# One pass for the gate mix, a normalised x kept in place, and the second layer norm on ScalarE from tile 3

## The reference, cut to what matters

```python
# x: (8, 512, 16, 16); tokens: 8 batches of 256, each of 512 channels
v = _ln_c(x)                                   # (x - mean) / sqrt(var + 1e-6), over a token's channels
xf = v.reshape(b, c, h * w)
u = stack([mean(xf), max(xf), std(xf, ddof=1)]) # per batch and channel
med = median(u.reshape(b, -1))                  # per batch
z = einsum('bck,ck->bc', (u - med) ** 3, cfc_w) / sqrt(1 + BN_EPS) * bn_w + bn_b
x = x + v * sigmoid(z)[:, :, None, None]        # the gate mix
t = tokens of x
h = _ln_t(t)                                    # the second layer norm, eps 1e-5
t = t + sum over the one chosen expert of sigmoid(logit) * glu(h, w1, v1, w2) + glu(h, shared weights)
```

## Time and profile before

| | us |
|---|---|
| time, median of 3 runs (414.07 to 414.93) | 414.22 |
| profiled execution, first to last instruction (span) | 411.6 |
| TensorE busy with matmuls in it | 385.1 |
| TensorE busy with weight loads | 303.8 |
| VectorE busy | 258.2 |
| ScalarE busy | 161.2 |
| GpSimd busy | 134.6 |

### The profile page before, as it was taken

The page is one execution under the profiler, slowest core; times in us unless marked ns, Lnnn a source line. Parts: engine busy times, 40 slices in busy tenths (PEclk is TensorE's granted clock), DMA queues, the critical chain, the costliest instruction groups (busy, mean ns, idle before and its releaser), DMA issues.

```text
span 411.6 us, 6789 instructions
## 1 busy us (share of the span) xinstructions
PE 385.1 (94%) x1982; PEld 303.8 (74%) x1986; DVE 258.2 (63%) x475; ACT 161.2 (39%) x274; POOL 134.6 (33%) x186
## 2 busy tenths in 40 slices
PE   5875659999999999999999999999999999999994
PEld 2442238888888788887888888888888888888883
DVE  6997876555857865656875557547375744676322
ACT  3996852223344324211116245153254515354110
POOL 7787811000100100005030245425535442446201
PEclk9998999999999999999999999999999999999999
DMA  8900502011201561140041469726546773752210
GB/s 321 397 2 0 204 1 78 27 51 60 90 30 53 187 247 53 53 153 27 32 133 41 128 217 323 282 98 256 204 134 219 294 258 118 262 182 71 86 37 30
DMA packets 14763, 55.96 MB, mean 136 GB/s; under 512 B 2575, under 2 KB 2575, under 8 KB 11280
## 3 DMA queue, kind: packets, MB, share of 16 engines
q1 hardware_dynamic: 9936, 40.93, 28.0%
q0 software_dynamic: 4800, 14.69, 10.0%
HBM read 43.02 MB, written 13.63 MB: 138 GB/s over the span
## 4 chain that ended last, share of the span: by engine, by line
PE 81%; DVE 7%; ACT 5%; issue 3%; POOL 2%; DMA 1%; DVEq 0%; POOLq 0%; ACTq 0%
PE GU L1255 47%; PE yb L1255 22%; PE th L1247 4%; PE tx L1240 4%; ACT tiles L534 2%; PE th L1284 2%; DVE search_junk L806 1%; ACT scratch L545 1%; ACT scratch L549 1%; DMA x_sb<-x_tok 1%; PE mb L1255 1%; DVE x_sb L864 1%; DVE tiles L862 1%; DVE bn_parts L871 1%; PE mb L1233 0%
## 5 line engine op out<-in xcount | busy, mean ns | idle before, releaser
L1255 PE MATMUL GU<-w_parts,xT 128*128 (+1 forms) x864 | 213.6, 395 | 0.0
L1255 PEld LDWEIGHTS GU<-w_parts,xT 128*128 128x128 f32 x864 | 158.3, 188 | 31.4
L1255 PE MATMUL yb<-w_parts,hT 128*128 (+1 forms) x420 | 102.6, 392 | 0.0
L1255 PEld LDWEIGHTS yb<-w_parts,hT 128*128 128x128 f32 x420 | 77.8, 188 | 15.7
L605 ACT ACTIVATE hT<-th 128x512 fp32r<-128x512 f32 x36 | 21.6, 599 | 170.8 <-PE th L1247 170.8
L472 POOL DMA_INDIRECT out<-x_sb,scatidx x20 | 37.6, 1879 | 92.5 <-DVE x_sb L1098 85.6
L922 DVE TENSOR_TENSOR w_parts<-w_raw,w_parts 128x2048 f32 (+1 forms) x24 | 54.9, 2288 | 7.4 <-issue 7.2
L907 DVE TENSOR_TENSOR hidden<-hidden,GU 128x512 f32<-128x512 f32 x36 | 24.8, 688 | 40.2 <-PE GU L1255 40.1
L522 ACT ACTIVATE w_parts<-w_raw 128x2048 f32 (+1 forms) x24 | 45.2, 1910 | 4.2 <-issue 3.9
L446 POOL TENSOR_TENSOR x_rstd<-x_mv,eps 128x1 f32<-128x1 f32 x16 | 3.0, 190 | 113.4 <-DVE x_mv L874 113.4
L901 DVE TENSOR_TENSOR hT<-th,hT 128x512 fp32r<-128x512 f32 x36 | 24.8, 689 | 23.9 <-ACT hT L605 23.6
(11 more groups left out here) (233 smaller groups left out, 339.8 us busy)
## 6 DMA issues: line engine op xcount, KB each, us to landing
w_raw<-weights SPq DMA_DIRECT2D x27, 1024.0 KB, 5.3
x_sb<-x_tok SPq DMA_DIRECT2D x8, 512.0 KB, 6.5
xn_d<-tiles SPq DMA_DIRECT2D x16, 256.0 KB, 2.0
z_d<-x_sb SPq DMA_DIRECT2D x16, 256.0 KB, 2.0
tiles<-xn_d,tokidx POOLq DMA_INDIRECT x20, 4.7
x_sb<-z_d,tokidx POOLq DMA_INDIRECT x20, 5.5
out<-x_sb,scatidx POOLq DMA_INDIRECT x20, 6.8
conv<-conv_par SPq DMA_DIRECT2D x1, 10.0 KB, 9.0
```

Source lines behind the costliest of these rows:

```text
L1255: last = pe.matmul(dst, left[:, lp, kc, :], wset(q, k, wp, kc), start=(i == 0), stop=(i == 3 * KC - 1))
```

## The change

`tok_std` = (var + eps) * rstd, the token's standard deviation, is a new small tile that GpSimd makes in `token_rstd`, behind `tok_shift`; a new semaphore `std_a` tells of it. `token_norm` writes the normalised tile over x itself instead of into the ring. Since x = v * std + mean, the mixed x less its mean is v * (gate + std): `mix_tile` is now one `scalar_tensor_tensor`, (gate row + std) * v. The mean does not matter to the second layer norm; it is added later, in `add_shared`, which becomes a `scalar_tensor_tensor` (yb + mean + x). The 16 `norm_a` of ScalarE are gone. The second norm of tiles 0 to 2 stays on VectorE; from tile 3 on it is an activation on ScalarE (scale rstd, bias -mean * rstd), for which GpSimd makes the bias (`x1_shift`, two more small instructions in each `rstd_tile`, and a wait on the new semaphore `x1_less`). In ScalarE's order the norm of `first` stands ahead of `h_hi(n)`, and that of the second tile behind `x_hi(first)`.

```diff
             def token_norm(b):
                 act.wait_ge(rstd_a, b + 1)
-                if b >= 2:
-                    act.wait_ge(aT_ready, b - 1)
                 for t in (2 * b, 2 * b + 1):
-                    act.activation(tiles[:, t % RING, :], x_sb[:, t, :], ACT.Identity, bias=tok_shift[:, t:t + 1],
+                    act.activation(x_sb[:, t, :], x_sb[:, t, :], ACT.Identity, bias=tok_shift[:, t:t + 1],
                                    scale=tok_rstd[:, t:t + 1]).then_inc(a_ready, 1)
...
-                own(pool.tensor_scalar(r, tok_mv[:, 2 * b:2 * b + 2, 1], LN_C_EPS, None, ALU.add))
-                own(pool.tensor_tensor(r, r, powers[:, 0, 0:2], ALU.pow))
+                std = tok_std[:, 2 * b:2 * b + 2]
+                own(pool.tensor_scalar(std, tok_mv[:, 2 * b:2 * b + 2, 1], LN_C_EPS, None, ALU.add))
+                own(pool.tensor_tensor(r, std, powers[:, 0, 0:2], ALU.pow))
                 pool.tensor_tensor(m, m, r, ALU.mult).then_inc(rstd_a, 1)
+                pool.tensor_tensor(std, std, r, ALU.mult).then_inc(std_a, 1)
...
             def rstd_tile(t, u):
                 pool.wait_ge(stats_b, t + 1)
-                r = x1_rstd[:, u:u + 1]
+                r, m = x1_rstd[:, u:u + 1], x1_shift[:, u:u + 1]
                 pool.tensor_tensor(r, x1_mv[:, u, 1:2], eps[:, 0:1], ALU.add).then_inc(x1_eps, 1)
+                if t < PREPARED_FIRST:
+                    pool.wait_ge(x1_eps, t + 1)
+                    pool.tensor_tensor(r, r, powers[:, 0, 0:1], ALU.pow).then_inc(rstd_b, 1)
+                    return
+                pool.tensor_scalar(m, x1_mv[:, u, 0:1], -1.0, None, ALU.mult).then_inc(x1_less, 1)
                 pool.wait_ge(x1_eps, t + 1)
-                pool.tensor_tensor(r, r, powers[:, 0, 0:1], ALU.pow).then_inc(rstd_b, 1)
+                pool.tensor_tensor(r, r, powers[:, 0, 0:1], ALU.pow).then_inc(x1_less, 1)
+                pool.wait_ge(x1_less, 2 * (t - PREPARED_FIRST + 1))
+                pool.tensor_tensor(m, m, r, ALU.mult).then_inc(rstd_b, 1)
...
-            def norm_a(t, u):
+            def norm_tile(t, u):
                 if t >= RING:
                     act.wait_ge(xn_out[u], 16 * (t // RING))
                     act.wait_ge(tx_done, t - RING + 1)
-                bias, scale = (v[:, t:t + 1] if isinstance(t, int) else v[:, ds(t, 1)] for v in (tok_shift, tok_rstd))
-                act.activation(tiles[:, u, :], tile_of(x_sb, t), ACT.Identity, bias=bias, scale=scale).then_inc(a_again, 1)
+                act.wait_ge(rstd_b, t + 1)
+                act.activation(tiles[:, u, :], tile_of(x_sb, t), ACT.Identity, bias=x1_shift[:, u:u + 1],
+                               scale=x1_rstd[:, u:u + 1]).then_inc(xn_ready, 1)
...
-            norm_a(0, 0)
-            norm_a(1, 1)
-            norm_a(2, 2)
-            norm_a(3, 3)
...
             for n in range(NT - 1):
                 now = PREPARED[n] if n < len(PREPARED) else ()
-                soon = PREPARED[n + 1] if n + 1 < len(PREPARED) else ()
+                for t in now[:1]:
+                    norm_tile(t, t % RING)
                 h_hi(n, n % 2)
                 silu_gate(n + 1, (n + 1) % 2)
                 for t in now[:1]:
                     x_hi(t, t % RING)
-                for t in soon:
-                    if t >= RING:
-                        norm_a(t, t % RING)
+                for t in now[1:]:
+                    norm_tile(t, t % RING)
...
             def mix_tile(t, u, batch):
-                buf, xt = tiles[:, u, :], tile_of(x_sb, t)
-                dve.wait_ge(a_again, t + 1)
+                xt = tile_of(x_sb, t)
+                dve.wait_ge(std_a, batch + 1)
...
-                dve.tensor_tensor(buf, buf, gate_rows(batch), ALU.mult).then_inc(gate_used, 1)
-                dve.wait_ge(gate_used, t + 1)
-                dve.tensor_tensor(xt, xt, buf, ALU.add).then_inc(x1_ready, 1)
+                dve.scalar_tensor_tensor(out=xt, in0=gate_rows(batch), scalar=tok_std[:, t:t + 1], in1=xt,
+                                         op0=ALU.add, op1=ALU.mult).then_inc(x1_ready, 1)
...
-                dve.tensor_tensor(xt, xt, yb[:, :], ALU.add).then_inc(y_used, 1)
+                dve.scalar_tensor_tensor(out=xt, in0=yb[:, :], scalar=tok_mv[:, t, 0:1], in1=xt,
+                                         op0=ALU.add, op1=ALU.add).then_inc(y_used, 1)
...
                 for t in held if n else ():
                     x_lo(t, t % RING)
-                norm_tile(first, first % RING)
                 take_logits(n, yb)
                 h_lo(n, n % 2)
                 for t in second:
                     gate_tile(t, t % RING, t // 2)
                 gated(n + 1, (n + 1) % 2)
                 x_lo(first, first % RING)
-                for t in second:
-                    norm_tile(t, t % RING)
```

More of the change, by code:

```diff
@@ L109, in program @@
         tok_shift = sb("tok_shift", [P, NT])
+        tok_std = sb("tok_std", [P, NT])
         x1_mv = sb("x1_mv", [P, RING, 2])
         x1_rstd = sb("x1_rstd", [P, RING])
+        x1_shift = sb("x1_shift", [P, RING])
         neg_mean = sb("neg_mean", [P, B, KC // 2])
@@ L155, in program @@
         rstd_a = sem("rstd_a")
+        std_a = sem("std_a")
         a_ready = sem("a_ready")
@@ L183, in program @@
         gates_spread = sem("gates_spread")
-        gate_used = sem("gate_used")
         warmed = sem("warmed")
-        a_again = sem("a_again")
         x1_ready = sem("x1_ready")
@@ L190, in program @@
         x1_eps = sem("x1_eps")
+        x1_less = sem("x1_less")
         stats_b = sem("stats_b")
@@ L346, in _ @@
                     sp.wait_ge(wlo, 3)
-                    sp.wait_ge(gate_used, STORED_GATES.stop * 2)
+                    sp.wait_ge(x1_ready, STORED_GATES.stop * 2)
                     load_w(1, DOWN)
@@ L1176, in _ @@
                     for k in range(KC):
-                        last = pe.transpose(aT[:, k, h * P:(h + 1) * P], tiles[:, t % RING, k * P:(k + 1) * P], ident[:, :])
+                        last = pe.transpose(aT[:, k, h * P:(h + 1) * P], x_sb[:, t, k * P:(k + 1) * P], ident[:, :])
                         if h and k == 1:
@@ L1227, in spread_gate @@
                 elif b == STORED_GATES.stop:
-                    pe.wait_ge(gate_used, 4)
+                    pe.wait_ge(x1_ready, 4)
                 else:
-                    pe.wait_ge(gate_used, 2 * b)
+                    pe.wait_ge(x1_ready, 2 * b)
                 bank = (th, tx)[b % 2] if b in STORED_GATES else mb
```

## The result

| | before | after |
|---|---|---|
| time, median (lowest to highest; 13 runs of each, side by side) | 414.04 us (413.33 to 414.93) | 414.63 us (413.99 to 416.62) |
| ratio after / before | | 1.0023, interval 1.0014 to 1.0033 |
| span of the first profiled execution | 411.6 | 413.6 |
| span of a second profile of the same kernel | 412.2 and 412.3 | 412.2 |
| VectorE, ScalarE, GpSimd busy (first profiles) | 258.2, 161.2, 134.6 | 243.6, 160.1, 140.1 |

The changed kernel is slower: by its medians 0.59 us or 0.14%, by the ratio of the runs 0.23%, with an interval that excludes 1. So it lies on the border between the two likeliest classes of the prediction, no change and slower, and 0.2 us from the forecast of 414.8.

A forecast was written before the change was run, and what follows sets the result against it. TensorE's products were taken to bound the kernel from about 63 to 406 us; 411.6 + 0.70 - 0.97 + 0.26 + 0.60 = 412.2, plus 2.6 from span to median, gave 414.8 us, range 414.2 to 415.5 (8 in 10: 413.7 to 416.2).

The forecast's parts named there:

- the two likeliest classes of the prediction: Whole kernel's time: within 0.2% (0.83 us) of the time before, chance 0.50; slower by more, 0.40.
- product in stage 1: Stage 1, GpSimd: the added tok_std product lengthens a full period, making token_norm(7) late; +0.70 us, bounds 0 and 1.38.
- passage behind the gates: 57 to 62 us, gates to first normalised tile: the one-pass mix brings TensorE's turn sooner; -0.97 us.
- tile 7's turn: Second tile in loop 3: longer norm chain through GpSimd and ScalarE makes its turn end later; +0.26 us.
- tile 11's turn: Second tile in loop 6: longer norm chain makes its turn start at 142.67 instead of 142.07; +0.60 us.
- the pair at 18.88: Stage 1: token_norm starts 0.04 after GpSimd's L410 ends and 0.09 after ScalarE's last read begins, two limits at once.
- Single tiles in a loop: Loops preparing one tile: h_lo ends before the down product, 0.3 us to spare in loops 6 and 10; cost zero.
- Half rate for the mix of the stored gates: Rival: mix of tiles 4 to 11 takes 1.25 us from two f32 SBUF sources; 416.8 us, chance 0.10.
- GpSimd's products at 0.30 each: Rival: small GpSimd instructions take 0.30, not 0.16, in stage 1 and both second tiles; 416.0 us, chance 0.18.
- Stage 1 hides the product: Rival: the statistics stage absorbs the added product and only the other terms hold; 414.1 us, chance 0.10.
- Shorter mix wins everywhere: Rival: stage 1 as before, VectorE freer, both second tiles in time; 412.9 us, chance 0.10.
- 2.6 us between span and median: Whole kernel: the median lies 2.6 us above the profiled span, kept in going from 412.2 to 414.8 us.

The follow-up runs named there:

- e1: Changed kernel with tok_std made in one GpSimd product for all 16 tiles behind the last standard deviation, not one a batch: 414.24 us, ratio 1.0009.
- e4: Changed kernel with one more small GpSimd product per batch in stage 1, its result unused: 415.88 us, ratio 1.004.
- e8: e5 with the mix of tiles 0 and 1 in two passes again: 415.06 us, ratio 1.0027 to the kernel before.
- e2: Changed kernel with ScalarE's norm of each loop's first tile behind h_hi and silu_gate instead of ahead of them: 414.12 us, ratio 1.0011.
- e6: Kernel before with seven further dummy products on TensorE during the median search: 414.0 us, ratio 0.9999.
- the dummies: Seven further TensorE products, results unused, that keep it busy while the median is searched; 414.11 us in the changed kernel, 414.0 in the kernel before.
- e5: Changed kernel with seven further dummy products on TensorE during the median search: 414.11 us, ratio 1.0003.
- e7: Changed kernel with one late tok_std product, the norm behind h_hi and silu_gate, and seven further dummy products: 412.72 us, ratio 0.9966.

## Why the prediction was right

By the profiles with an undisturbed passage the terms are:

| term | forecast | measured | from |
|---|---|---|---|
| product in stage 1 | +0.70 | +0.65 | gates' activation 56.40, 57.05; e1 takes it back, e4 doubles it |
| passage behind the gates | -0.97 | -0.95 | 5.53, 4.58; e8 gives +0.96 back |
| tile 7's turn | +0.26 | +0.15 | ends at 111.47, 111.32, with -0.30 carried in |
| tile 11's turn | +0.60 | +0.47 | starts at 142.07, 142.39, with -0.15 carried in |
| wait at 376 us | none | +0.36 | lag 0.30, then 0.66 |
| sum | +0.59 | +0.68 | spans 411.6, 412.2: +0.6 |

All measured terms are from the first profile of the kernel before and the second of the changed one. That pair is among the fastest of each kernel. With the excess of the passage taken off (0.47, 0.46 and 1.47), the spans are 411.6, 411.7 and 411.8 before and 412.1 and 412.2 after, so that the change costs 0.3 to 0.6 us inside the span, and the sum of 0.68 lies a little above that.

**Stage 1** went as worked out: GpSimd's period 3.32, `token_norm` 0.04 behind L413, each period paid. (0.17 + 4 x 0.13 is 0.69, which the prediction wrote as 0.70.) The reading that carried it was the pair at 18.88: two limits ended together, and e1 and e4 show that GpSimd's is a real one.

**The passage**: every distance held (aggregate 1.65 behind the mix, forecast 1.66; norm 60.94 against a forecast of 60.28 + 0.65).

**The second tiles** are the terms that were mis-sized, too high. From the aggregate to the turn the forecast had 7.65 (7.05 + 0.60), measured 7.54. GpSimd's chain took 1.17 (103.38 to 104.55), not 1.29: the independent step stands at 0.15 and the pow 0.18 behind it, where I had 0.30. The hand-over to ScalarE took 0.12 instead of 0.04. Twice -0.12 and twice +0.08 is -0.08 of the -0.11. The step as a mechanism holds: e2 moves only the norm and both waits go.

**Single tiles in a loop** cost nothing, as said: in loop 6 `h_lo` ends at 137.73 + 0.69 = 138.42 and the down product starts at 138.81, in loop 10 these are 181.01 and 181.38. The spare was put at 0.3 and is 0.4.

**The rivals.** Half rate for the mix of the stored gates: false, 743 ns with either operand. The Trainium skill (Vector Engine (DVE) Microarchitecture Reference, "Points that are easy to get wrong") says that this form with two non-bf16 SBUF sources has half the throughput; at 128 x 512 in f32 this trace shows no such thing. GpSimd's products at 0.30 each: false, 0.15. Stage 1 hides the product: false. Shorter mix wins everywhere: false with this order of ScalarE; with the norm behind `h_hi` (e2) the second tiles do come in time.

One thing in the forecast's range, 414.2 to 415.5, does not add up: its upper end has GpSimd's steps at 0.30 in stage 1 only (1.38 instead of 0.70). With them in stage 3 too it is 416.0, as the prediction's own rival says.

**What the sum left out** are two things that together are as large as its terms. The first is VectorE's late read at 365 us and the wait at 376 us that follows from it. The second is the clock: I put 2.6 us between span and median and called it launch and end. In the 13 profiled executions whose own time is known it is 1.92 to 1.99 (413.56 - 411.6 in e6, 415.57 - 413.6 in the first profile after); the rest is that other executions are longer inside. An execution of the kernel before like the first profile would take 411.6 + 1.95 = 413.55, and its median is 414.04. So part of the agreement is luck, and 414.8 came close by a base that was too plain: the second profile of the changed kernel has 412.2 and 414.15, and the median of 414.63 lies 0.48 above it. With the dummies the two kernels differ by 414.11 - 414.0 = 0.11 only, with an uncertainty in each ratio of 0.0009 (0.4 us); the four measured terms alone give +0.32, all five +0.68. Of the e5 and e6 profiles only e5's is typical of its kernel (414.17 in a median of 414.11); e6's was the fastest of its twelve executions (413.56 in a median of 414.0), and what the others lose was not traced. What share of the +0.59 the clock has can't be told closer than that, and that it equals the forecast to the hundredth is chance.

**A version that beats both.** e7's kernel (one late product, norm behind `h_hi`, dummies) was measured twice: 412.72 and 412.80, 1.1 to 1.2 us below the kernel before (0.9966 and 0.997, both intervals below 0.9985). It keeps the -0.95 of the passage and pays neither the product nor the turns; VectorE's late read it still pays.

## What to carry to other kernels

Before an instruction is added to an engine, however small, compare that engine's period with the sum of its steps: here one product recorded at 0.19 us, put into a full period, cost 0.65 by batch 7, and the same work behind the loop cost nothing in stage 1. When a step moves to another engine, its place in that engine's order is half of the change: the norm ahead of `h_hi` delayed two turns, behind it none. And profile the same kernel more than once before its span is taken as the base of a sum.

## What the runs showed of the hardware that I had not expected

- TensorE's granted clock in 55 to 60 us was 1.00, 0.66 and 0.71 in three profiles of the kernel before and 0.50 and 1.00 in two of the changed one. TensorE had been busy for 2.3 to 2.7 of the 5 us ahead in these five; in the five profiles of kernels with the dummies it had been busy for 3.65 to 4.0, and the clock was 1.00. What decides it in a given execution stays open.
- A three-operand VectorE pass over 128 x 512 f32 takes 743 ns whether its second tensor is in PSUM or SBUF.
- GpSimd issues independent products of 128 x 1 or 128 x 2 every 0.15 us though each is recorded as 0.19 long.
- VectorE's queue reads a table entry from the tile `scratch` ahead of a branch. That read took 0.75 to 0.94 us, and the work behind the branch started 0.87 to 0.89 us after its end. Beside it a pause of 0.42 us with no releaser stood in nine of ten profiles of kernels with the change and in none of the four without it, though the code around it is the same.
